# Last pass of a chunked recurrence: transposes written as products with the identity, and the products on ones taken out

## The reference

```
xn = layernorm(x)
O_lh, O_rh = polar_orthogonal(W_lh), polar_orthogonal(W_rh)      # 12 rounds of X = 1.5 X - 0.5 X X^T X
q = xn @ Wq^T ; v = xn @ Wv^T
h_t = rms(h_(t-1) @ O_lh^T + q_t @ O_rh^T)      # 512 steps in order, rms(z) = z / sqrt(mean(z^2) + 1e-6)
attn = (h * v) @ Wc^T
ffn = sqrt((xn @ cos(theta + theta_noise))^2 + (xn @ sin(phi + phi_noise))^2)
out = x + attn + ffn
```

## Time and profile before

| | us |
|---|---|
| median of 3 runs | 161.42 |
| the runs | 161.51, 160.47, 161.42 |
| the profiled execution's own time | 158.67 |
| its span, first to last instruction | 156.9 |
| its mean granted TensorE clock | 0.937 of full speed |

### The profile page before, as it was taken

One profiled execution on the slowest core, in us unless ns is written; L12 is line 12 of the kernel. 1 busy time (PEld: TensorE's weight loads), 2 busy tenths in 40 slices (PEclk: granted clock), 3 DMA queues, 4 the chain that ended last, 5 costly groups with the idle time before them and its releaser, 6 DMA issues.

```text
span 156.9 us, 2766 instructions
## 1 busy us (share of the span) xinstructions
PE 119.8 (76%) x767; PEld 94.8 (60%) x767; DVE 94.3 (60%) x410; ACT 83.9 (53%) x307; POOL 56.2 (36%) x94
## 2 busy tenths in 40 slices
PE   6888888746977787889998866499986886877730
PEld 6666777735865675566665634477775775766510
DVE  3599999723442545555565563255578788888730
ACT  3146999975445666766867657133334344344300
POOL 7106778500010135655463563422223323323300
PEclk9999999999999999999999999755599999999975
DMA  4980000000000000000000000001010210110210
GB/s 120 267 298 3 0 6 0 0 0 4 0 0 2 0 0 0 4 0 0 0 2 2 2 0 0 4 0 53 14 67 0 73 67 2 67 67 4 102 34 10
DMA packets 3347, 5.00 MB, mean 32 GB/s; under 512 B 448, under 2 KB 1344, under 8 KB 3328
## 3 DMA queue, kind: packets, MB, share of 16 engines
q1 hardware_dynamic: 3024, 4.46, 8.4%
q0 software_dynamic: 160, 0.26, 0.5%
q10 hardware_dynamic: 144, 0.07, 0.1%
HBM read 2.69 MB, written 2.10 MB: 31 GB/s over the span
## 4 chain that ended last, share of the span: by engine, by line
PE 48%; DVE 26%; ACT 11%; issue 7%; POOL 3%; DVEq 1%; ACTq 0%; POOLq 0%
PE bank L896 8%; DVE W L664 8%; PE bank L904 7%; PE bank L853 6%; PE bank L768 4%; DVE WMID L647 3%; PE bank L863 3%; PE bank L812 3%; DVE SQM L652 3%; DVE bank L658 3%; PE bank L798 3%; PE bank L905 3%; PE bank L885 2%; DVE WTM L671 2%; PE bank L763 2%
## 5 line engine op out<-in xcount | busy, mean ns | idle before, releaser
L853 PE MATMUL bank<-IDENT,W 128*128 128x128 f32 x33 | 11.2, 340 | 14.7 <-DVE W L664 14.2
L293 POOL TENSOR_TENSOR FS<-FSQ 128x256 f32<-128x256 f32 x16 | 11.7, 733 | 27.5 <-ACT FSQ L429 27.5
L647 DVE SCALAR_TENSOR_TENSOR WMID<-UZ,RT,bank 128x129 f32<-128x129 f32 x33 | 11.6, 350 | 16.6 <-PE bank L904 14.4
L410 ACT ACTIVATE SQE<-W 128x129 f32<-128x129 f32 x35 | 10.9, 313 | 18.5 <-DVE W L664 18.5
L853 PEld LDWEIGHTS bank<-IDENT,W 128*128 128x128 f32 x33 | 4.7, 143 | 24.0 <-DVE W L664 24.0
L896 PE MATMUL bank<-WCT,PV 128*128 128x128 f32 x64 | 16.4, 343 | 2.7 <-POOL PV L324 2.7
L768 PE MATMUL bank<-ONES 128*128 128x128 bf16 x157 | 18.0, 237 | 0.0
L281 POOL TENSOR_SCALAR XN<-X,MV,RSTD 128x128 f32<-128x128 f32 x16 | 13.5, 846 | 11.7 <-DVE RSTD L569 11.7
L633 DVE COPY WT<-bank 128x128 f32<-128x128 f32 x33 | 9.6, 291 | 12.0 <-PE bank L853 12.0
L446 ACT ACTIVATE SQM<-WMID 128x129 f32<-128x129 f32 x16 | 5.0, 314 | 22.0 <-DVE WMID L647 22.0
L875 PE MATMUL bank<-CS,XNT 128*128 128x256 f32 x64 | 16.5, 380 | 0.0
(11 more groups left out here) (151 smaller groups left out, 272.3 us busy)
## 6 DMA issues: line engine op xcount, KB each, us to landing
X<-in_L_attn_x_dram SPq DMA_DIRECT2D x8, 256.0 KB, 5.9
out_dram<-OUT SPq DMA_DIRECT2D x7, 256.0 KB, 2.0
out_dram<-OUT SPq DMA_DIRECT2D x2, 128.0 KB, 1.7
WP<-in_L_attn_W_rh_dram ACTq DMA_DIRECT2D x1, 64.0 KB, 2.0
WP<-in_L_attn_W_lh_dram SPq DMA_DIRECT2D x1, 64.0 KB, 2.3
ANG<-in_L_ffn_theta_dram POOLq DMA_DIRECT2D x1, 64.0 KB, 3.7
WV<-in_L_attn_Wv_dram SPq DMA_DIRECT2D x1, 64.0 KB, 3.5
ANG<-in_L_ffn_phi_dram POOLq DMA_DIRECT2D x1, 64.0 KB, 3.5
```

Of the source, the lines that this page charges most:

```text
L647: dve.scalar_tensor_tensor(out=WMID[:, 0:E], in0=UZ[:, uz(j), 0:E], scalar=norm_of(m), in1=YB[:, 0:E], op0=ALU.mult, op1=ALU.add).then_inc ...
L853: pe.transpose(TB[:, 0:P], state(s)[:, 0:P], IDENT[:, :]).then_inc(t_done, 1)
```

## The change

In the last pass every transpose of a state (`TM`, and `TB` for the states s > GUESSES but those that end a pass before the last) is an ordinary product with the identity as the moving operand. The value is the same. All `fill` products go, with their tile of ones and its memset, and `keep_warm` waits for one tile of ones in place of two. The order of the rest is as before.

```diff
-        ONES16 = sb("ONES16", [P, P], BF16)
...
             dve.memset(ONES[:, :], 1.0).then_inc(S["ones_ready"], 1)
-            dve.memset(ONES16[:, :], 1.0).then_inc(S["ones_ready"], 1)
...
-            def fill(n):
-
-                for _ in range(n):
-                    pe.matmul(FILL[:, 0:P], ONES16[:, :], ONES16[:, :], start=True, stop=True)
-
-            pe.wait_ge(S["ones_ready"], 2)
+            pe.wait_ge(S["ones_ready"], 1)
             keep_warm(6)
...
+                elif s > GUESSES:
+                    pe.matmul(TB[:, 0:P], W[:, 0:P], IDENT[:, :], start=True, stop=True).then_inc(t_done, 1)
                 else:
                     pe.transpose(TB[:, 0:P], state(s)[:, 0:P], IDENT[:, :]).then_inc(t_done, 1)
...
                 if m >= GUESSES:
                     if j:
                         projected(j - 1)
-                        fill(3)
                     else:
                         pe.wait_ge(S["v_copied"], BATCHES)
                     pe.wait_ge(mid_ready, m + 1)
-                    pe.transpose(TM[:, 0:P], WMID[:, 0:P], IDENT[:, :]).then_inc(tm_done, 1)
-                    fill(3)
+                    pe.matmul(TM[:, 0:P], WMID[:, 0:P], IDENT[:, :], start=True, stop=True).then_inc(tm_done, 1)
                 transposed(m + 1)
...
                 if m >= GUESSES:
                     projected(j)
-                    fill(4)
```

More of the change, by code:

```diff
@@ L9 @@
 F32 = mybir.dt.float32
-BF16 = mybir.dt.bfloat16
 I32 = mybir.dt.int32
```

## The result

| | before | after |
|---|---|---|
| median, us | 160.94 (the three runs of before and one taken with the changed kernel) | 164.97 |
| the runs, us | 161.51, 160.47, 161.42, 158.32 | 165.11, 164.82, 176.53, 164.82 |
| span of the profiled execution, us | 156.9 | 163.3 |
| its mean granted clock | 0.937 | 0.873 |

The changed kernel takes 1.0346 times as long, 95% interval 1.0179 to 1.0514: slower for certain, by 2% or more not for certain. The execution of 176.53 us had a mean granted clock of 0.666 and is not in the ratio. In a later measurement the same kernel took 162.28 us where the kernel before took 159.40.

The account below looks back on a forecast made before the run. The last pass was taken as one chain (L904, `WMID`, `W`, transpose, `WT`, L904), partly at the lower clock. Terms +1.9 + 0.2 - 0.1 = +2.0 us; +1.9 was put on the median 161.42, giving 163.3 us, range 158.7 to 173.0.

Parts of the forecast that it names:

- case A: Last pass: low-clock stretch as long as before, within a move or two; 163.3 us (161.5 to 165.5), chance 0.40.
- rival B: Last pass: low clock stays to the end (172.7 us) or returns late (half way about 167); chance 0.27.
- the sum: All terms together, if the clock does what it did: +2.0 us, bounds +0.5 and +2.6.
- `TB` at full clock: State's transpose made a product, with nothing covering it: +0.16 us per move, +1.9 us for 12 moves.
- `TM` at full clock: Middle state's transpose made a product, covered by ScalarE's root: +0.01 to 0.02 us per move, +0.2 us in all.
- Fills at full clock: Taking the fills out of the last pass's full-clock moves: 0, bounds 0 and -0.4 us for 12 moves.
- Low-clock moves: Last pass: fills out -0.65 us, two products +0.61, about 0 per move; -0.1 us for three moves.
- The handover: Move into the last pass: two products end some 0.3 us later, covered by TensorE's wait for GpSimd's `PV`: 0.
- The start: `keep_warm` no longer waits for the second memset: at most 0.1 us off, taken as 0.
- The length of the low stretch: Time at the lower clock in the last pass: 13 us before, forecast low for some 14 us.
- Rival C: Handover: clock does not fall, as products may count as work where transposes may not; 157.3 us, chance 0.20.
- The gap between the profiled 158.67 and the median of 161.42: Kernel before: 2.75 us, nearly two more lower-clock moves at 1.2 us each, which would pay nothing for the product.

Follow-up runs that it names:

- double transposes: Kernel before with 36 products on ones at the handover, no fills in the moves, each of a move's two transposes made twice: 157.33 us, ratio 0.986.

## Why the prediction was right

Slower was forecast, 163.3 us in a range of 158.7 to 173.0; 164.97 came. The direction came for the two reasons that were named, the products' price at full clock (case A) and a longer low stretch (rival B). But the case on which 163.3 rests, A, did not come: I had written that it is wrong if the low stretch changes by more than two moves, and it did. That 164.97 lies within A's own range of 161.5 to 165.5 is partly luck, since the sum was put on a median of 161.42, which the kernel before did not reach again (159.57, 158.82, 159.40). Between the two profiled executions the sum was +2.0 us, and +6.4 came: +1.9 before the last pass, mostly by chance, +4.0 in its moves and +0.5 behind them.

- **`TB` at full clock, +0.16:** right, 3.03 to 3.04 us a move, and 3.03 for that product alone.
- **`TM` at full clock, +0.01 to 0.02, under ScalarE's root:** right in the change. Alone it cost 0.13, by a path that I had not followed: GpSimd's `PV`, L896 and the fills behind it. The full clock's term of +0.16 to 0.17 a move holds for the pair, 3.03 to 3.05 us with or without the fills.
- **Fills at full clock, 0:** right as a delay (2.87 us a move with fills and without). Incomplete as a cost, because I had named no other work of theirs. With transposes they are what holds the clock.
- **Low-clock moves, "about 0 per move, and 4.05 us":** 3.95, with -0.7 for the fills (forecast -0.65) and +0.58 for the products (forecast +0.61).
- **The handover, 0:** wrong by a little. The state's product is covered, the middle one costs 0.15 us, because the wait named as its cover ends later too.
- **The start, 0:** right. `keep_warm` begins at 1.05 us in place of 1.19, but the first product of the orthogonal rounds behind it stands at 6.49 and 6.26 in the changed kernel's two executions and at 6.30 before.
- **The length of the low stretch:** mis-sized. Case A kept it at some 14 us, give or take two moves; it was 27.3 us in both profiled executions. Three moves more were low, and they cost +3.1 us where the sum had +0.5 for them at full clock. That is why the 15 moves together came out at +4.0 and not at +2.0; the first move's -0.6 took part of it back. This is rival B's mechanism, less work in a low move, at its half-way size ("about 167"): with the same two products, but the fills kept, the stretch was 10.2 us. The execution at a mean clock of 0.666 does not fit B's end. It was low for some 117 of its 174.7 us, and from the handover to the end are only some 74, so it must have been low for long before the last pass too. There is no trace of it.
- **Rival C, the clock does not fall at the handover:** it fell in both profiled executions. Its premise, that transposes are not seen by the clock, was refuted by double transposes.
- **The gap between the profiled 158.67 and the median of 161.42:** I took it for two more moves at the lower clock. Those runs have no clock on record. In a later measurement the kernel before's executions of 160.8 us and more were low for 22.6 to 26.9 us altogether and those under 158.7 us for 16.0 to 19.4, so the lower clock is at least part of such a gap.

What sets the length of a low stretch stays open. With one profiled execution each, it was 6.8, 10.2, 13.7 and 13.7 us in kernels with the fills, 27.3 twice with products alone, and to the end with transposes alone. The kernels with the fills, which have the most work in a low move, came back first, and the one with the least did not come back. Among those with fills the order does not follow the work (6.8 us with the state's product, 13.7 with the middle one, 10.2 with both, 13.7 with neither), and other executions of the same kernel had other lengths; no rule was shown.

## What to carry to other kernels

Idle-time work that costs nothing may still be what keeps the clock: before taking it out, or pricing it at zero, run the kernel with the waits filled and see whether the clock survives without it. To stop a fall, put cheap products where the engine waits long, here 36 of them in a 2.3 us wait for 2% (0.8 to 3.2%), and not more work on the chain. A float32 product with the identity is a transpose for 0.16 us more behind a wait at full clock, and it should not stand on a chain.

## What the hardware showed that was not expected

- The clock also fell in the middle of a steady loop, at 117.5 us, after five moves of 2.87 us at full clock.
- Once low, moves with single transposes and no fills (3.37 us) stayed low for 50 us; with products (3.95 us) the clock came back after 27.3 us in the two profiled executions.
- Single transposes let the clock fall and double ones held it, with TensorE's busy time at 11.66 and 12.33 us of the same 16.5 us.
- The same code lost the clock at 33 us in one kernel's execution and kept it in another's; that alone was worth 2.0 us.
- Behind `FLAG`, VectorE's last result, lie 4.6 to 5.5 us of the span in eleven profiled executions and 2.1 us in one. A gain of 3 us there has nothing to do with the change under study, and the median alone does not show it.
